# Hopfield retrieval in a two-layer kernel: the pairs of heads of a round divided anew between GpSimd, ScalarE and VectorE

## The reference

```python
def entmax15(x):
    x = (x - jnp.max(x, -1, keepdims=True)) / 2.0
    ...
    tau_star = jnp.take_along_axis(tau, support - 1, -1)
    return jnp.square(jnp.clip(x - tau_star, 0.0, None))
...
for _ in range(NUM_STEPS):
    scores = jnp.einsum('bhsd,hnd->bhsn', xi, K) * beta
    w = entmax15(scores)
    xi = jnp.einsum('bhsn,hnd->bhsd', w, V)
out = xi.transpose(0, 2, 1, 3).reshape(B, S, H * hd) @ Wo.T
```

## Time and profile before

| | |
|---|---|
| median of 3 runs | 1899.72 us (1896.36 to 1903.34) |
| the profiled execution | 1899.34 us, its span 1897.6 us |
| TensorE busy | 1666.5 us, 88% |
| VectorE busy | 1467.5 us, 77% |
| ScalarE busy | 1234.3 us, 65% |
| GpSimd busy | 697.4 us, 37% |
| granted TensorE clock, mean | 0.927 |

### The profile page before, as it was taken

How to read it: one execution, slowest core, us unless ns; L and a number is a source line. 1 busy time by engine, 2 the same in 40 slices (tenths; PEclk the granted TensorE clock), 3 DMA queues, 4 the chain that set the end, 5 groups by cost and what they waited for, 6 DMA issues and landing times. The chain is left out here.

```text
span 1897.6 us, 31938 instructions
## 1 busy us (share of the span) xinstructions
PE 1666.5 (88%) x10554; PEld 1155.0 (61%) x10554; DVE 1467.5 (77%) x3080; ACT 1234.3 (65%) x2769; POOL 697.4 (37%) x1326
## 2 busy tenths in 40 slices
PE   4949899999999888788779998888876899987999
PEld 3537544444544467677668876766754455545888
DVE  7767789999997258999997869999445789826655
ACT  3633477788778433788986768888752588865322
POOL 2002222222222215666675646666232111224632
PEclk9979799999999889888989999899987799988999
DMA  3464133223330200000000000000037223110000
GB/s 123 147 208 67 34 68 66 55 52 68 69 69 2 76 1 1 1 1 1 1 1 1 1 1 1 1 1 1 1 111 183 42 55 67 36 68 7 12 12 23
DMA packets 36996, 82.27 MB, mean 43 GB/s; under 512 B 9952, under 2 KB 12384, under 8 KB 35936
## 3 DMA queue, kind: packets, MB, share of 16 engines
q1 hardware_dynamic: 36832, 80.22, 16.8%
HBM read 52.53 MB, written 27.26 MB: 42 GB/s over the span
## 5 line engine op out<-in xcount | busy, mean ns | idle before, releaser
L1165 ACT ACTIVATE probs<-pss 128x512 f32<-128x512 f32 (+3 forms) x1152 | 482.0, 496 | 127.2 <-PE pss L1128 125.9
L873 DVE TENSOR_REDUCE negmax<-px 128x2 f32<-128x1024 f32 (+2 forms) x480 | 508.4, 1114 | 44.3 <-PE px L855 41.3
L1722 POOL TENSOR_SCALAR rp<-sw,tau 128x256 f32<-128x256 f32 x720 | 341.8, 505 | 7.1
L1232 POOL TENSOR_SCALAR_AFFINE_SELECT probs<-probs 128x512 f32<-128x512 f32 x192 | 120.4, 635 | 505.3 <-ACT probs L1165 505.3
L1128 PE MATMUL pss<-queries,keys 64*128 64x512 f32 (+3 forms) x1152 | 294.9, 395 | 5.5 <-ACT probs L1165 4.3
L855 PE MATMUL px<-keys,queries 63*128 63x512 f32 (+3 forms) x1152 | 266.0, 419 | 10.5 <-DVE negmax L873 10.5
L1128 PEld LDWEIGHTS pss<-queries,keys 64*128 64x128 f32 x1152 | 167.1, 190 | 152.4 <-ACT probs L1165 136.5
L1142 PE MATMUL po<-probs,vals 128*32 128x512 f32 (+3 forms) x2304 | 248.1, 507 | 0.3 <-POOL probs L1232 0.2
L1571 PE MATMUL pss<-again,sw 128*128 128x256 f32 x1024 | 244.5, 397 | 0.0
L1876 DVE BATCH_NORM_STATS2 st<-rp 128x6 f32<-128x512 f32 x360 | 229.9, 677 | 2.3 <-POOL rp L1722 2.3
L1571 PEld LDWEIGHTS pss<-again,sw 128*128 128x128 f32 x1024 | 203.4, 203 | 28.6
(11 more groups left out here) (375 smaller groups left out, 2556.4 us busy)
## 6 DMA issues: line engine op xcount, KB each, us to landing
queries<-rec_q SPq DMA_DIRECT2D x96, 128.0 KB, 3.3
keys<-rec_k SPq DMA_DIRECT2D x96, 128.0 KB, 3.4
queries<-rec_q SPq DMA_DIRECT2D x96, 64.0 KB, 3.3
keys<-rec_k SPq DMA_DIRECT2D x96, 64.0 KB, 3.2
rec_q<-fs SPq DMA_DIRECT2D x16, 256.0 KB, 4.2
rec_k<-fs SPq DMA_DIRECT2D x16, 256.0 KB, 4.6
rec_q<-vals SPq DMA_DIRECT2D x16, 256.0 KB, 3.0
rec_k<-vals SPq DMA_DIRECT2D x16, 256.0 KB, 3.7
```

The costliest lines, as they stand in the source:

```text
L873: return e.tensor_reduce(out, from_px, X_AXIS, ALU.max, negate=True)
L1165: e.activation(tl.probs[arg][:, w, :], tl.pss[scores % 3][:, 512 - width:512], ACT.Exp).then_inc(self.exp_made, 1)
L1722: x = e.tensor_scalar(self.rp[rp % 6][:, :, h], self.view(g, q)[:, h, :], -BIG, self.tau[r][:, 2 * q + h:2 * q + h + 1], ALU.min, ALU.max)
```

## The change

Pair 0 of each round is now done by ScalarE alone (`WHOLE = 1`): two clips into tiles `ends`, each with the sum of its results written beside (`accum_out`, into the place of the mean in `st`), then two squares of them into tiles `square`, again with their sums, straight into `z`. Pair 1 is clipped by ScalarE for VectorE as before (`BY_ACT = 2`), and GpSimd clips pairs 2 to 7, six instead of five. VectorE takes seven statistics a round, and waits for the sums (`totals_made`) before each step; it scales them to a mean by one small operation per step. Five `ra` tiles are left. The hand-written orders are the same.

```diff
@@ -1441,7 +1441,7 @@
 
 
     CHAINS, GROUPS, STEPS, ROUNDS = 4, 2, 3, 3
-    BY_ACT = 3
+    WHOLE, BY_ACT = 1, 2
     ACT_ORDER, PE_ORDER = "Jcdtttstsrt2ss1ttastsbss0", "ttttatbtttxcdR"
     PAIRS = 8
     RESULTS = (((0,) * 8 + (8,), (1,) * 8 + (6,), (1,) * 8 + (6,), (1,) * 8 + (8,), (1,) * 8 + (4,)),
@@ -1461,9 +1461,10 @@
             self.xn = [k.sb("xn", [P, D]) for _ in range(2)]
             self.xt = [k.sb("xt", [P, 2, DC, P]) for _ in chains]
             self.sw = [k.sb("sw", [P, 2, HH, NM]) for _ in range(self.CHAINS + 1)]
-            self.ra, self.rp = [k.sb("ra", [P, NM, 2]) for _ in range(7)], [k.sb("rp", [P, NM, 2]) for _ in range(6)]
+            self.ra, self.rp = [k.sb("ra", [P, NM, 2]) for _ in range(5)], [k.sb("rp", [P, NM, 2]) for _ in range(6)]
             self.top = [k.sb("top", [P, 16, 8]) for _ in chains]
             self.sums = k.sb("sums", [P, 16, 8])
+            self.ends_at, self.square = [k.sb("ends", [P, NM]) for _ in range(2)], [k.sb("square", [P, NM]) for _ in range(2)]
             self.st, self.z, self.neg, self.step = (
                 [k.sb(n, [P, *shape]) for _ in range(2)] for n, shape in (("st", (3, self.PAIRS, 6)), ("z", (3, 16)),
                                                                          ("neg", (4, 16)), ("step", (3, 16))))
@@ -1482,6 +1483,7 @@
          self.joint_root, self.move_made, self.next_move_made) = k.sems(
             "least_made first_made joint_made first_asked joint_asked first_root joint_root move_made next_move_made")
         self.summed, self.spread_made, self.pool_steps = k.sems("summed spread_made pool_steps")
+        self.clipped, self.totals_made = k.sems("clipped totals_made")
 
     def tile(self, g, i):
         return 2 * (g % 4 + 4 * (g // 12)) + i
@@ -1616,16 +1618,32 @@
 
     def act(self, e):
         e.drain()
-        ra = 0
+        ra, whole = 0, 0
 
         def relus(g, r, q, n):
             self.wait_negated(e, g, r)
-            if n >= 7:
-                e.wait_ge(self.ra_read, n - 6)
+            if n >= 5:
+                e.wait_ge(self.ra_read, n - 4)
             for h in range(2):
-                x = e.activation(self.ra[n % 7][:, :, h], self.view(g, q)[:, h, :], ACT.Relu,
+                x = e.activation(self.ra[n % 5][:, :, h], self.view(g, q)[:, h, :], ACT.Relu,
                                  bias=self.negated(g, r)[:, 2 * q + h:2 * q + h + 1])
             x.then_inc(self.ra_made, 1)
+
+        def totals(g, r):
+
+            nonlocal whole
+            self.wait_negated(e, g, r)
+            par = (g + 1 + r) % 2
+            if whole:
+                e.wait_ge(self.totals_made, whole)
+            for h in range(2):
+                e.activation(self.ends_at[h][:], self.view(g, 0)[:, h, :], ACT.Relu, bias=self.negated(g, r)[:, h:h + 1],
+                             accum_out=self.st[par][:, r, 0, 3 * h + 1:3 * h + 2]).then_inc(self.clipped, 1)
+            for h in range(2):
+                e.wait_ge(self.clipped, 2 * (whole // 2) + h + 1)
+                e.activation(self.square[h][:], self.ends_at[h][:], ACT.Square,
+                             accum_out=self.z[par][:, r, h:h + 1]).then_inc(self.totals_made, 1)
+            whole += 2
 
         def first_root(g):
             e.wait_ge(self.first_asked, g + 1)
@@ -1660,7 +1678,8 @@
         def relu_pairs(g, r):
             nonlocal ra
             if 0 <= g < self.n:
-                for q in range(self.BY_ACT):
+                totals(g, r)
+                for q in range(self.WHOLE, self.BY_ACT):
                     relus(g, r, q, ra)
                     ra += 1
 
@@ -1759,22 +1778,26 @@
         e.wait_ge(self.spread_made, g + 1)
         e.tensor_reduce(self.negated(g, 0), self.sums[:], X_AXIS, ALU.min).then_inc(self.least_made, 1)
 
-    def first_step(self, e, g, step, read_a, read_p):
+    def first_step(self, e, g, step, read_a, read_p, totals):
 
         now, then = (g + 1) % 2, g % 2
         st = self.st[now][:, 0].rearrange("p q (h s) -> p (q h) s", h=2)
         m, z, neg = st[:, :, 1], self.z[now][:, 0], self.neg[now][:, 0]
         m2, root, rec, move = self.m2[0][:, 0], self.root[0][:, 0], self.rec[0][:, 0], self.step[then][:, 0]
         by_pool = slice(2 * self.BY_ACT, None)
+        whole, parts = slice(0, 2 * self.WHOLE), slice(2 * self.WHOLE, None)
         e.wait_ge(self.ra_read, read_a)
         e.wait_ge(self.rp_read, read_p)
+        e.wait_ge(self.totals_made, totals)
+        step(e.tensor_scalar(m[:, whole], m[:, whole], 1.0 / NM, None, ALU.mult))
         at = step(e.tensor_tensor(m[:, by_pool], m[:, by_pool], neg[:, by_pool], ALU.add))
         yield
         e.wait_ge(self.math, at)
         at = step(e.tensor_tensor(m2, m, m, ALU.mult))
         yield
         e.wait_ge(self.math, at)
-        e.scalar_tensor_tensor(z, m2, 256.0, st[:, :, 2], ALU.mult, ALU.add).then_inc(self.first_asked, 1)
+        e.scalar_tensor_tensor(z[:, parts], m2[:, parts], 256.0, st[:, parts, 2], ALU.mult,
+                               ALU.add).then_inc(self.first_asked, 1)
         yield
         step(e.reciprocal(rec, m))
         for _ in range(4):
@@ -1788,7 +1811,7 @@
         e.wait_ge(self.math, at)
         e.scalar_tensor_tensor(self.neg[then][:, 1], move, -1.0 / NM, neg, ALU.mult, ALU.add).then_inc(self.first_made, 1)
 
-    def joint_step(self, e, beat, step, read_a, read_p):
+    def joint_step(self, e, beat, step, read_a, read_p, totals):
 
         n, part, now, then = beat - 1, self.joint(beat), beat % 2, 1 - beat % 2
         rounds, later = slice(1 + part.start, 1 + part.stop), slice(2 + part.start, 2 + part.stop)
@@ -1801,8 +1824,11 @@
         move, new_move, new_neg = self.step[now][:, part], self.step[then][:, rounds], self.neg[then][:, later]
         m2, root, rec, inv, w, y = (t[:, part] for t in (self.m2[1], self.root[1], self.rec[1], self.inv, self.w, self.y))
         by_pool = slice(2 * self.BY_ACT, None)
+        whole, parts = slice(0, 2 * self.WHOLE), slice(2 * self.WHOLE, None)
         e.wait_ge(self.ra_read, read_a)
         e.wait_ge(self.rp_read, read_p)
+        e.wait_ge(self.totals_made, totals)
+        step(e.tensor_scalar(m[:, :, whole], m[:, :, whole], 1.0 / NM, None, ALU.mult))
         at = step(e.tensor_tensor(m[:, :, by_pool], m[:, :, by_pool], neg[:, :, by_pool], ALU.add))
         if part.start == 0:
             e.wait_ge(self.move_made, beat - 1)
@@ -1815,7 +1841,7 @@
         step(e.scalar_tensor_tensor(w, m, 2.0, m_old, ALU.mult, ALU.add))
         yield
         e.wait_ge(self.math, at)
-        at = step(e.scalar_tensor_tensor(z, m2, 256.0, squares, ALU.mult, ALU.add))
+        at = step(e.scalar_tensor_tensor(z[:, :, parts], m2[:, :, parts], 256.0, squares[:, :, parts], ALU.mult, ALU.add))
         yield
         e.wait_ge(self.math, at)
         at = step(e.tensor_tensor(y, z_old, z, ALU.subtract))
@@ -1855,7 +1881,7 @@
         e.drain()
         k = self.k
         step = Steps(self.math)
-        self.bn_a, self.bn_p = 0, 0
+        self.bn_a, self.bn_p, wholes = 0, 0, 0
         e.wait_ge(self.loaded, 32)
         e.wait_ge(self.consts, 18)
 
@@ -1865,11 +1891,11 @@
 
         def moments(g, r, between):
             st = self.st[(g + 1 + r) % 2][:, r]
-            pool, act = range(self.BY_ACT, self.PAIRS), range(self.BY_ACT)
+            pool, act = range(self.BY_ACT, self.PAIRS), range(self.WHOLE, self.BY_ACT)
             for q in [*pool, *act] if r != 1 else [*act, *pool]:
                 if q < self.BY_ACT:
                     e.wait_ge(self.ra_made, self.bn_a + 1)
-                    e.bn_stats(st[:, q, :], self.ra[self.bn_a % 7][:].rearrange("p n h -> p (n h)")).then_inc(self.ra_read, 1)
+                    e.bn_stats(st[:, q, :], self.ra[self.bn_a % 5][:].rearrange("p n h -> p (n h)")).then_inc(self.ra_read, 1)
                     self.bn_a += 1
                 else:
                     e.wait_ge(self.rp_made, self.bn_p + 1)
@@ -1908,6 +1934,7 @@
             rounds = {r: g for g, r in self.rounds(beat)}
             w = beat if beat < self.n else None
             if 2 in rounds:
+                wholes += 2
                 moments(rounds[2], 2, late)
             finish(late)
             if 1 <= beat <= self.n:
@@ -1915,10 +1942,11 @@
             for tile in self.ADDS_EARLY.get(beat, ()):
                 result(*tile)
             if 1 in rounds:
+                wholes += 2
                 moments(rounds[1], 1, iter(()))
             for tile in self.ADDS_MID.get(beat, ()):
                 result(*tile)
-            joint = self.joint_step(e, beat, step, self.bn_a, self.bn_p) if 2 <= beat <= self.n + 2 else iter(())
+            joint = self.joint_step(e, beat, step, self.bn_a, self.bn_p, wholes) if 2 <= beat <= self.n + 2 else iter(())
             if w is not None:
                 largest(w, 0, 0, joint)
             if self.begins(beat + 1):
@@ -1931,7 +1959,8 @@
             finish(joint)
```

(3 more changed lines are left out.)

## The result

The changed kernel takes **1911.13 us** (median of 5 runs, 1909.31 to 1913.14), the kernel before 1899.72 (1896.36 to 1903.34). The ratio on record is 1.0049, with a 95% interval of 1.0031 to 1.0067: slower by 0.3 to 0.7%. (The plain quotient of the two medians is 1.0060, inside that interval.) Forecast were 1918 us and a range of 1900 to 1934. The direction and the mechanism came as forecast, the size did not: the profiled span grew from 1897.6 to 1907.3 us, by 9.7 where the sum gave 19.1.

A forecast was written before the change was run, and what follows sets the result against it. VectorE's loop with ScalarE was taken to bound the even beats, the loop through TensorE close behind. Even beats +17.4 us, transposed-state beats +1.5, fill -1, end +1.2: +19.1 us, forecast 1918 us, range 1900 to 1934.

The forecast's parts named there:

- VectorE's loop: Even beats: ScalarE's cuts, root, 19.9 us of VectorE, next cuts; claimed to have almost no slack.
- the loop through TensorE: Even beats: ScalarE's cuts, relus and squares, TensorE's last turn, 32 matmuls, last score copy; ends at t+23.9.
- A: ScalarE: price of one sum (accum_out), taken as 0.14 us, bounded between 0 and 0.3.
- D: ScalarE: what a round costs more, 4A - 0.18, taken as 0.38 us.
- t+11.04 + 2D: When VectorE's first statistic of round 1 can start, t+11.8, counted from the start t of the beat's first cut.
- From the pair to the next cut: VectorE's path from round 1's first statistic to the next cut: 13.96, less 0.59, plus 0.25 and 0.2, 13.82 us.
- The other beats: Outside the even beats: transposed-state beats +1.5 us together, TensorE-bound stretch nothing, pipeline fill -1.
- The end: Pipeline's end: VectorE's wait for round 1's relus +1.2 us after the saving; TensorE's backlog of results +1.2 counted.
- Rival 4: GpSimd's six pairs become the bound if a clip grows by a tenth; chance counted with (3).
- (1): Sums cost next to nothing, A up to 0.05: 1895 to 1908 us, no measurable change; chance 0.22.
- Rival (2): Faster: VectorE's relief reaches the threshold, 0.3 to 0.8 us a beat gained, 1887 to 1894 us; chance 0.10.
- (3): Much slower: A 0.25 to 0.3 or squares wait for clips, 1930 to 1940 us; chance 0.18.

The follow-up runs named there:

- the two runs that take the wait away: The changed kernel with ScalarE's relus ahead of its sums, 1899.81 us; or with VectorE reading GpSimd's six pairs first in round 1 too, 1904.08 us.
- the other order: ScalarE's round 0 behind the joint root, last score copy behind two cuts and first root: changed kernel with relus first 1912.02 us, kernel before 1919.48.

## Why the prediction held, and where its size was off

**What bounds the kernel: right.** The three relations of the timeline account for the kernel after, for the two runs that take the wait away and for the later round 1; the runs with sums in all rounds, with the earlier round 1 and with the other order needed more than them. They are VectorE's loop, the loop through TensorE 0.35 us behind it, and ScalarE's part of round 1 with a margin of 1.0 us. VectorE's share of 97% alone would have promised a gain.

**The wait of VectorE in round 1: right in place and cause, 0.8 us too long.** Forecast was 2.1 us, measured 1.28; it stands in each of the 14 even beats, 18.7 us together. VectorE's own path up to it shrank by less than the 0.59 counted. It asks for the pair at 815.9, t+10.1, where t+9.7 was forecast; the threshold of the first step (L1812), which stands on that path, takes 0.37 us there instead of 0.15, because GpSimd, with its longer clipping, is still at work beside it. This shortened the wait and cost nothing. (The scan takes 0.72 instead of 0.41, but the product before it 0.19 instead of 0.46; together they are as long as before.)

**The sum's price: the term that was mis-sized.** A was taken as 0.14, from the rows of the two roots; it is 0.09. D is 0.17, not 0.38. The pair is read at t+11.35, and t+11.04 + 2D is 11.38: the formula is right, the term in it was too large by 0.42 us a beat, 5.9 us of the 8.8 by which the even beats stayed below their 17.4. The bound from the whole tiny ACTIVATE of 0.20 us came close to the instruction's length (0.19 to 0.20) but not to its price. The squares did not wait for their clips, as assumed.

**From the pair to the next cut: right in this beat, too long in most.** This makes up the other 3 us or so. Forecast 13.82 us, measured 13.80 (817.20 to 831.00). The later beats show what of it is contention. Two beats on, ScalarE's first cut and VectorE's rows:

```profile
855.81 2.51 ACT L1674 ACTIVATE sw<-sw,neg 128x256 f32<-128x256 f32 x6 [0.48 <-DVE neg L1878]
```

```profile
867.17 0.69 DVE L1898 BATCH_NORM_STATS2 st<-ra 128x6 f32<-128x512 f32 x1 [1.27 <-ACT ra L1628]
...
872.77 0.23 DVE L1841 SCALAR_TENSOR_TENSOR w<-st 128x32 f32<-128x32 f32 x1
```

The next cut starts at 880.63, 13.46 us after 867.17: L1841 takes 0.23 us here and 0.55 in the beat at 805.85. So the scaling and GpSimd together cost 0.1 us in such a beat, where 0.45 was counted, and 0.43 in the other kind. With D = 0.17 and these two values the formula gives 24.85 and 25.18; measured are 24.82 and 25.15. The 14 beats average 24.99. L1841 takes 0.54 or 0.55 us in five of them, and these are the five that take 25.1 us or more.

**The other beats: two terms too large.** The beats with a transposed state and the TensorE-bound stretch together came out 0.2 us shorter, not 1.5 longer; the fill gained 0.1, not 1. These two misses, 1.7 and 0.9 us, have opposite signs and partly cancel in the sum. The end cost 1.4, forecast 1.2; there VectorE's longest wait for the relus is 2.9 us, and the two terms of that forecast were not told apart.

**GpSimd: right.** Twelve clips take 5.67 us, and VectorE never waits for it in the 14 even beats. Its share of VectorE's waits is 3.5 us over the whole execution, against 2.3 in the kernel before. Rival 4 is out.

**The rivals.** The nearest was (1): its condition, a sum of up to 0.05 us, was not met, and the kernel is slower than its 1908. The prediction's line of 0.5% was too coarse, though: the ratio on record lies just inside it, at 1.0049, and its interval still tells the kernel from the one before. Rival (2) needed the pair before about t+10.4; the swap of the relus delivers it in time, and the beat still stays at 24.3 by the loop through TensorE, which has the measured D of 0.17 in it. Its 0.3 to 0.8 us a beat were given for a D of about 0, which no run tested in this loop. The remark under (3) on TensorE's clock did not matter here (0.90 against 0.91), because the loop through TensorE had room, but it added to the time of two runs in which that loop became the bound, those with sums in all rounds and with the earlier round 1.

## What to carry to other kernels

A relief of the busiest engine counts only up to the next loop: before moving work, add up every loop that passes the same beat, and look at what stands last on the engine that takes the work over, for one consumer's operand put behind four new operations cost more here than the whole relief brought. Where an engine makes things for two readers, write first what is read first. A price that no row shows is better estimated from how soon successors start (0.11 and 0.14 us here, 0.09 measured) than from how long an instruction lasts (0.20).

## What the runs showed of the hardware

- On ScalarE a sum beside an activation is an instruction of its own, 0.19 to 0.24 us long in the rows here, and it delays the next by 0.09 to 0.10 us (pitch of the relus 0.50 with sums and 0.40 without). The Trainium skill, VectorE: DVE Perf Modes, "Two Vector instructions with no wait between them", states for VectorE that an operation which also writes its accumulator is two instructions; the runs show the same for ScalarE.
- Some of VectorE's small operations with two inputs in SBUF are longer beside GpSimd's work. The threshold L1789 has a median of 0.15 us in the kernel before and of 0.37 where GpSimd has a sixth pair. Of the root's product and the scan behind it, one or the other is long in the two beats shown: 0.46 and 0.41 us before, 0.19 and 0.72 after, with 0.71 and 0.75 us from the product to the next statistic. (In two of the even beats of the kernel before both are.) Statistics and maxima, with one input, kept their 0.68 and 0.41.
- TensorE's matmuls behind an idle time can be much slower, but the length of that time does not tell when. With sums in all rounds, 32 matmuls took 8.76 us after 1.14 and 0.65 us of idling (granted clock of the stretch 0.76, between the two levels of 1.2 and 2.4 GHz), and 7.07 after 1.62 and 0.65 in the next beat (1.00). In the kernel before, 16 took 5.78 us at 834.34 behind an idle time of 2.31 us and two shorter ones (0.72, 0.19), and 3.62 at 932.01 behind one of 2.61 and two shorter ones (0.71, 0.65).
